# Delta rule: the write strengths (beta) taken from stored rows instead of a projection in each step

## The reference, cut to what matters

```python
h = rmsnorm(x, norm_in_w)
h = silu(depthwise_conv(h) + conv_b)
q, k, v = h @ q_w, h @ k_w, h @ v_w          # 16 heads of 64, q and k then normed
alpha = sigmoid(h @ alpha_w + alpha_b)       # one per head and channel
beta = sigmoid(h @ beta_w + beta_b)          # one per head
def step(s, inp):
    qt, kt, vt, at, bt = inp
    s = s * at[..., None]
    u = einsum('bhd,bhdv->bhv', kt, s)
    s = s + bt[..., None, None] * (kt[..., None] * (vt - u)[..., None, :])
    return s, einsum('bhdv,bhd->bhv', s, qt)
```

## Time and profile before

| | us |
|---|---|
| median of 3 runs | 5169.21 |
| lowest and highest | 5156.3, 5171.2 |
| span of the profiled execution | 5145.8 |

### The profile page before, as it was taken

The page is one execution under the profiler, slowest core; times in us unless marked ns, Lnnn a source line. Parts: engine busy times, 40 slices in busy tenths (PEclk is TensorE's granted clock), DMA queues, the critical chain, the costliest instruction groups (busy, mean ns, idle before and its releaser), DMA issues. The chain is left out here.

```text
span 5145.8 us, 181702 instructions
## 1 busy us (share of the span) xinstructions
PE 3922.1 (76%) x73332; PEld 3131.2 (61%) x73332; DVE 2953.6 (57%) x8172; ACT 1773.9 (34%) x4061; POOL 2629.7 (51%) x3000
## 2 busy tenths in 40 slices
PE   4779973674068888888888888888886679588695
PEld 2534443664047676766677676767674479477595
DVE  5832267755556665656556566656555645488723
ACT  3732231442023333333333333333333134211163
POOL 2310016514546666666666666666664242477644
PEclk8989986886579999999999999999998889799797
DMA  0030003664000000000000000000000056200154
GB/s 22 2 138 0 0 3 95 190 181 121 23 15 14 11 14 11 14 11 14 11 11 14 11 14 11 14 11 14 11 14 8 18 208 229 87 1 1 61 187 125
DMA packets 129703, 249.33 MB, mean 48 GB/s; under 512 B 24672, under 2 KB 60656, under 8 KB 127344
## 3 DMA queue, kind: packets, MB, share of 16 engines
q1 hardware_dynamic: 98224, 178.93, 11.0%
q0 software_dynamic: 16384, 33.59, 2.2%
q10 hardware_dynamic: 14400, 26.22, 1.4%
HBM read 178.89 MB, written 59.77 MB: 46 GB/s over the span
## 5 line engine op out<-in xcount | busy, mean ns | idle before, releaser
L2597 POOL TENSOR_TENSOR e_kd<-e_kd,e_tail 128x512 f32<-128x512 f32 x325 | 368.9, 1135 | 587.2 <-PE psum L2709 586.7
L2739 PE MATMUL psum<-e_T,e_N 64*64 64x32 f32 x10400 | 402.3, 228 | 71.3 <-remote 34.8
L2739 PEld LDWEIGHTS psum<-e_T,e_N 64*64 64x64 f32 x10400 | 363.3, 141 | 100.7 <-issue 99.7
L2709 PE MATMUL psum<-e_kd,e_k 64*64 64x64 f32 x10400 | 396.7, 228 | 28.6 <-DVE e_AT L3127 28.4
L729 POOL DMA_INDIRECT m_back<-m_rows_out,m_idx x256 | 253.3, 990 | 295.8 <-DVEq L1169 121.5
L2709 PEld LDWEIGHTS psum<-e_kd,e_k 64*64 64x64 f32 x10400 | 361.2, 143 | 37.3 <-issue 37.1
L3133 DVE COPY e_Z<-psum 64x256 f32<-64x256 f32 x325 | 135.8, 418 | 386.0 <-PE psum L2739 384.2
L3022 ACT ACTIVATE e_T<-psum 128x256 f32<-128x256 f32 x325 | 125.9, 387 | 631.1 <-PE psum L2760 631.1
L723 POOL DMA_INDIRECT rows_in<-xn,m_idx x256 | 256.0, 1000 | 145.5 <-issue 76.2
L840 PE MATMUL psum<-m_rowsT,m_w 128*128 128x128 f32 x2304 | 317.3, 297 | 3.0 <-DVE m_h L1145 2.3
L2760 PE MATMUL psum<-e_Z,e_TT 64*64 64x32 f32 x8320 | 297.6, 222 | 26.7 <-DVE e_Z L3133 21.2
(11 more groups left out here) (464 smaller groups left out, 10744.4 us busy)
## 6 DMA issues: line engine op xcount, KB each, us to landing
m_w<-in_m_w SPq DMA_DIRECT2D x88, 516.0 KB, 5.7
m_w<-in_m_w SPq DMA_DIRECT2D x224, 129.0 KB
m_rows<-rows_in SPq DMA_DIRECT2D x100, 256.0 KB, 3.8
m_rows_out<-m_out ACTq DMA_DIRECT2D x100, 256.0 KB, 2.1
m_w<-in_m_w SPq DMA_DIRECT2D x88, 259.0 KB, 3.6
e_w<-in_e_w SPq DMA_DIRECT2D x66, 321.0 KB, 3.0
rows_in<-xn SPq DMA_DIRECT2D x6, 2048.0 KB, 23.4
m_wd<-in_m_wd SPq DMA_DIRECT2D x3, 2048.0 KB, 8.1
```

Of the source, the lines that this page charges most:

```text
L2597: return g.tensor_tensor(both_odd(dst[:], m), both_odd(src[:], m), gate.unsqueeze(1).broadcast_to((P, 2, nb, m)), ALU.mult)
L2709: r = pe.matmul(c.psum[half(h), G_, chunk(u)], keys[half(h), chunk(u)], both_odd(gated[half(h), :, chunk(u)], 1 << l), start=True, stop=True)
L2739: r = pe.matmul(c.psum[half(1 - h), Z_, u * HC:(u + 1) * HC], N[half(h), l - 1, chunk(u)], even(T[half(h), chunk(u)], 1 << l), start=True, ...
```

## The change

- The beta columns, repeated 64 times, and their bias leave the weights that each step loads. `project_gate(1)` and `gate_beta()` are gone from the step. The wait for `sums_read` that `project_gate(1)` had goes to `head_sums`; in the part in front of the loop it stands ahead of a projection, and a wait for `al_read` ahead of `project_v`.
- Stage d also computes beta as 16 rows (heads) by 4096 columns (tokens): one more 512-column product and one Identity for each batch, one Sigmoid over all at the end, and two stores to DRAM from ACT's queue, which ACT waits for before the stage ends.
- In each step SP waits for `be_free`, which DVE gives once L3198 has read `be`, and issues two DMAs, each of which reads one row of 512 numbers and writes it to 64 partitions. Only then comes the wait for `w_free` and the load of `W`.

```diff
-WCOLS = 5 * P + 2
+WCOLS = 4 * P + 1
@@ stage_delta_in, tensor
+            def beta_rows(b):
+                i = b % 2
+                if b >= 2:
+                    pe.wait_ge(br_read[i], 1)
+                    pe.sem_clear(br_read[i])
+                pe.matmul(c.ps[i][0:2 * NPAIR, :], bw[:], c.xT[:, b * L:(b + 1) * L], start=True, stop=True).then_inc(br_ps[i], 1)
...
                 betas(b)
+                beta_rows(b)
@@ stage_delta_in, scalar
+                a.activation(br[:, b * L:(b + 1) * L], c.ps[i][0:2 * NPAIR, :], ACT.Identity, bias=bbr[:]).then_inc(br_read[i], 1)
...
                 silu(b)
+                if b:
+                    beta_rows(b - 1)
+            beta_rows(B - 1)
+            a.drain()
+            a.activation(br[:], br[:], ACT.Sigmoid).then_inc(br_ready, 1)
+            a.wait_ge(br_ready, 1)
+            a.sem_clear(br_ready)
+            for h in range(2):
+                a.dma_start(c.be_rows[:, h * L:(h + 1) * L].rearrange("(a b) n -> a b n", b=B),
+                            br[h * NPAIR:(h + 1) * NPAIR, :].rearrange("a (b n) -> a b n", b=B)).then_inc(be_stored, 16)
             a.wait_ge(b_ready, 1)
             a.sem_clear(b_ready)
             a.activation(c.beta[:], bt[:].rearrange("p (t h) a -> p a t h", h=2), ACT.Sigmoid)
+            a.wait_ge(be_stored, 32)
@@ stage_delta, sync
+            sp.wait_ge(core.lasting_sem("beta_stored"), 32)
+            for h in range(2):
+                sp.dma_start(be[half(h), :], c.be_rows[0:1, h * L:(h + 1) * L].broadcast_to((DH, L))).then_inc(be_ready, 16)
             with sp.Fori(0, LAST + 1) as i:
+                sp.wait_ge(be_free, 1)
+                sp.sem_clear(be_free)
+                for h in range(2):
+                    sp.dma_start(be[half(h), :], c.be_rows[bass.ds((i + 1) % LAST, 1), h * L:(h + 1) * L].broadcast_to((DH, L))).then_inc(be_ready, 16)
                 sp.wait_ge(w_free, 1)
@@ stage_delta, tensor
-            def project_gate(n):
-                if n:
-                    pe.wait_ge(sums_read, 1)
-                    pe.sem_clear(sums_read)
-                pe.matmul(c.ps[Q_ + n][:], W[:, (2 + n) * P:(3 + n) * P], hs[:], start=True, stop=True).then_inc(ab_ps, 1)
+            def project_gate():
+                pe.matmul(c.ps[Q_][:], W[:, 2 * P:3 * P], hs[:], start=True, stop=True).then_inc(ab_ps, 1)
...
                 state_and_output(2)
-                project_gate(1)
                 from_state(3)
@@ head_sums, after its wait for kq_pe
+                pe.wait_ge(sums_read, 1)
+                pe.sem_clear(sums_read)
@@ stage_delta, scalar
-            def gate_beta():
-
-                a.wait_ge(ab_ps, 2)
                 a.sem_clear(ab_ps)
-                a.activation(be[:], c.ps[K_][:], ACT.Sigmoid, bias=W[:, 5 * P + 1:5 * P + 2]).then_inc(be_ready, 1)
...
                 t_copy(3)
-                gate_beta()
                 u_copy()
@@ stage_delta, vector, normed_keys
-                v.wait_ge(be_ready, 1)
+                v.wait_ge(be_ready, 32)
                 v.sem_clear(be_ready)
                 ch.link(v.scalar_tensor_tensor(kqn[:, 0, :], kn[:], -1.0, be[:], ALU.mult, ALU.mult))
+                v.sem_inc(be_free, 1)
```

## The result

| | before | changed |
|---|---|---|
| median, us | 5162.76 (4 runs) | 5268.89 (4 runs) |
| lowest to highest | 5151.66 to 5171.2 | 5261.53 to 5282.24 |
| span of the profiled execution | 5145.8 | 5269.7 |

The changed kernel takes 1.0217 of the time before (95% interval 1.0197 to 1.0237), 106 us more by the medians. The forecast was 5271 us.

A forecast was written before the change was run, and what follows sets the result against it. PE, though busiest, was taken to wait on DVE's S, with steps lengthened by half-clock stretches. Span 5145.8 + 9 (stage d) + 93 (clock) = 5247.8 us, plus 23.4 to the median gives 5271; range 5176 to 5350.

The forecast's parts named there:

- The matmul gains nothing: Beta's matmul in the step: PE waits for DVE's S anyway, stall 0.99 to about 2.04 us, gain 0.
- The first rival: PE bounds the step, so removing the matmul brings L2828 earlier by its length: 5105 us, chance 0.06.
- The clock behind it: Behind beta's removed matmul: emptier PE loses clock, 0.65 more half-clock stretches a step at 2.2 us, 93 us in all.
- The sum: Whole kernel: profiled span 5247.8 us with stage d and clock losses, plus 23.4 to the median, 5271 us.
- The rule on idle gaps: Skill page's rule: only idle gaps longer than any wait of this loop cost clock, so the change would cost none.
- The second rival: The 2 us hole costs no clock, or new falls replace those behind the sums: 5178 us, chance 0.16.
- Beta's Sigmoid: Removed from ACT in each step, 0.69 us: nothing won, because ACT waits for PE again before L3029.
- The row loads: Two a step on SP's queue ahead of the load of W, readers far off: costed at nothing.
- the third rival: Row loads land so late that DVE waits at L3198: 5308 us with stage d, chance 0.02.
- Stage d: Ahead of stage e: the added beta products, Identity, Sigmoid and stores cost 9 us, between 6 and 14.
- What would show it: Signs in the new profile: L2828 waits some 2 us, loop clock 0.92 to 0.93, mean step about 38.5, stage e near 1461.
- whole steps at full clock, 35.0 us: Sign in the loop: steps that keep full clock still last 35.0 us after the change.

The follow-up runs named there:

- e2: Kernel before with only beta's matmul removed from the 65 steps, Sigmoid and all else kept: ratio 1.016 to the kernel before.
- e1: Changed kernel with an unread 512-column product put back in the place of beta's matmul: 5527.24 us, 1.0065 of the kernel before.
- e8: Changed kernel with an unread 256-column product put in the place of beta's matmul: 5547.57 us, 1.0075 of the kernel before.
- e5: Changed kernel with DVE's list reordered so that S, masked(4) and residual(3) precede norms(): 5122.31 us, 0.9939 of the kernel before.
- e9: Changed kernel with S first on DVE, state_and_output(3) and project_v ahead of key_norms, masked(5) ahead of normed_keys: 1.0174 of the kernel before.
- e3: Changed kernel with the two row loads taken out of the loop and issued only in front of it: 1.0156 of the kernel before.
- e4: Kernel before with two row loads added to each step, into a tile that nobody reads: 1.0013 of the kernel before.
- e0: Changed kernel measured again, unaltered, in another group of runs: 5617.2 us, 1.0214 of the kernel before.

## Why the prediction was right, point by point

**The matmul gains nothing.** Right. The stall grew from 0.99 to 1.99 us (forecast 2.04), DVE's chain to S did not move, and e2 shows the same without anything else changed. The first rival (PE bounds the step, 5105 us) fell with it.

**The clock behind it.** The mechanism is shown from four sides: e2 (hole alone), e1 and e8 (hole filled), e5 (hole closed by DVE) and e9 (hole opened elsewhere). The size came out right by two errors against each other. The forecast had 0.65 stretches more a step at 2.2 us each, 93 us. Measured are 119 stretches instead of 54, 1.0 more a step, for 103.3 us of loop, so 1.6 us a stretch at most. More of them: 73 more behind S, where 34 of 43 falls lasted 6.83 us (two stretches), which the forecast had only in its upper bound, and 15 fewer behind the sums. Cheaper: on the way from S to the next writing of S there are 264 us more at half clock for the 121.5 us, 0.46 us for each. That a slow PE costs less where it would have waited may be a part of this, but the price of 2.2 was too high to begin with. It was taken against the two steps of 34.75 and 35.10 us, which are among the quickest: the 23 steps of the kernel before without half clock last 35.56 us in the mean, and the 30 with one stretch 37.35, so 1.8 us a stretch and 0.52 for each us. By that price the loop before loses nearer 100 us to the clock than 124. Between the loads and the clock the 103.3 us cannot be parted exactly, as e3 and e4 show, so the price is an upper bound.

**The sum.** That 5271 came within 2 us of 5269 is luck. The forecast span of the profiled execution was 5247.8 us and the measured one is 5269.7, 22 us more: 7.7 from ahead of the change, 3.4 in stage d and 10.3 in the loop. The 23.4 us that were added for the median made up for it. That term was the distance of one profiled execution from the median of its kernel, and for the changed kernel it is -0.8.

**The rule on idle gaps.** The second rival would have had 5178 us. The kernel is at 5269 with waits of at most 2.0 us at that place, and e5 wins it back by making that wait 0.4 us. The Trainium skill, page "TensorE: Matmul & The Clock Gate", section "Why this matters for your kernels", ties losses of clock in the middle of a kernel to idle gaps between bursts of matmuls. The prediction said that no wait of this loop is of that length, and there it misread the trace. Four waits of PE in the kernel before, in the last step of a loop body, last 3.0 to 3.6 us. The first of them:

```profile
1962.47 1.15 PE L2709 MATMUL psum<-e_kdn,e_kn 64*64 64x64 f32 x32 [3.28 <-remote]
```

In each of the four, or at most 1.4 us behind it, the clock falls, so there the trace agrees with the rule. It does not cover the other falls. For the place of the change the measurement decides: waits well below what the page warns of, among small matmuls, were enough.

**Beta's Sigmoid.** Right as far as it shows: 36 us less of ACT in the loop (883.91 to 847.85) and no step shorter for it.

**The row loads.** They land in 3.0 us, the load of W in 3.4 instead of 3.0, and DVE never waits for them; the third rival fell. "Costed at nothing" is not borne out, but hardly refuted: e4 gives 7 us (-1 to 15), e3 32 us with an uncertainty of about 20. How they cost time, if they do, is open.

**Stage d.** Forecast + 9 within 6 to 14, measured + 12.4. The Sigmoid of 4096 columns took 3.62 us (forecast 3.8). What was missed is the tail: the two issues of the store took 2.09 us of ACT's queue ahead of the last Sigmoid, and the stage ended 3.3 us behind that one (1469.11 to 1472.41), where before it was 0.25.

**What would show it.** Clock 0.92 (forecast 0.92 to 0.93), mean step 38.75 us (38.5), stage e at 1472 instead of 1461, 7.7 us of it from ahead of stage d. The falls behind S begin 0.1 to 3.2 us behind its start, so 1.7 to 4.8 us behind the end of L2857 (L2815 before), as forecast (1.5 to 5). One sign did not hold: whole steps at full clock, 35.0 us, were not to be found. The 8 steps of the changed kernel without half clock last 36.9 us or more, where the kernel before has 23 that go down to 35.0. The row loads do not make this: e2 and e3 have none of the change's in their steps, and their 6 and 5 steps of this kind last 36.8 and 36.7 us or more, while e5 has the loads and 23 such steps from 34.2 on. Nor is the way behind S longer at full clock (24.86 us against 24.85, above). So the few steps that escape the fall seem to be those that are longer for another reason; part of it is short pauses inside groups of matmuls, which the trace puts down to no engine and which the kernel before has too. Why just these escape stays open.

## What to carry to other kernels

Before taking a matmul away, look at what PE waits for next: if the wait's releaser does not hang on the matmul, it was free, and it may have been keeping the clock. If it has to go, close the hole that it leaves, best by giving the waiting instruction's input sooner on the other engine (e5: 2.7% of the changed kernel's time for one reordered list), else by dead work (e1, e8). When orders are changed, read the clock along with the waits, since a gain of 1 us in one wait can open a hole of 1.3 us in another place and lose more (e9).

## What the runs showed of the hardware

- The clock fell behind a place of 4 to 5 us with a wait of 2 us and small matmuls, 77 stretches in 64 steps. It kept up with 0.7 us of a wide product in the wait, of which 1.4 us were left (e8, 2 stretches), and with a wait of 0.4 us and no wide product (e5, none).
- Behind that place it mostly stayed at 1.2 GHz for 6.83 us (34 of 43 falls), behind the sums mostly for 3.41 (18 of 22).
- The four waits of 3.0 to 3.6 us in the loop before each had a fall of the clock in them or at most 1.4 us behind.
- A us at half clock cost about 0.5 us: 0.46 behind S in the changed kernel, 0.52 in the kernel before.
- The changed kernel took 5269 us in one group of runs and 5617 in another (e0), with loops alike within 0.3% (2479.7 and 2485.4 us). The stages in front of the loop ended at 1529 and 1678 us, and those behind it took 1261 and 1444. Whether the chip or something else makes this is not shown.
